# A new order for the third norm and the router, and for the convolution's modulation and value products

## The reference

```python
mod = (_silu(c) @ wmod).reshape(B, 6, 1, -1)
h = _layernorm(x, axis=-1) * (1 + ca) + sa
x = x + ga * block(h)        # ga, gb: sign kept, magnitude at least 0.25
```

```python
stats = concat([x.mean, x.std(ddof=1), x.min, x.max, norm2(x), (abs(x) < 1e-6).mean])
h = gelu(concat([xf, stats]) @ r1_w.T + r1_b)
probs = softmax(h @ r2_w.T)   # then top 2 of 32, capacity per expert
```

## Time and profile before

| | |
|---|---|
| median of 3 runs | 1381.84 us (1379.79 to 1382.64) |
| the profiled execution | 1385.09 us, span 1383.3 us |
| PE busy | 1188.5 us, 86% of the span |
| DVE, ACT, POOL busy | 922.5, 887.2, 577.3 us |
| granted TensorE clock, mean | 0.927 of full |
| first stage (norm and convolution) | 0 to 43.5 us |
| third norm and router up to its logits | 102 to 138.4 us |

### The profile page before, as it was taken

One profiled execution on the slowest core, in us unless ns is written; L12 is line 12 of the kernel. 1 busy time (PEld: TensorE's weight loads), 2 busy tenths in 40 slices (PEclk: granted clock), 3 DMA queues, 4 the chain that ended last, 5 costly groups with the idle time before them and its releaser, 6 DMA issues.

```text
span 1383.3 us, 30358 instructions
## 1 busy us (share of the span) xinstructions
PE 1188.5 (86%) x11444; PEld 713.8 (52%) x11444; DVE 922.5 (67%) x2432; ACT 887.2 (64%) x2384; POOL 577.3 (42%) x554
## 2 busy tenths in 40 slices
PE   7788038757999999999979899997899978899978
PEld 5334037753555555555534566663566643466643
DVE  3454852137989889889863699896566744666733
ACT  3564001115777777777867788885699862799961
POOL 1022024634444444444331132232788820888820
PEclk8897557979999999999999999999899999999998
DMA  9002014541000000000021122220011100011100
GB/s 335 3 0 61 9 61 134 185 125 39 1 1 1 1 1 1 1 1 1 1 107 34 45 74 71 75 79 32 16 29 29 29 15 0 22 27 25 29 14 31
DMA packets 30271, 60.36 MB, mean 44 GB/s; under 512 B 5379, under 2 KB 17163, under 8 KB 29486
## 3 DMA queue, kind: packets, MB, share of 16 engines
q1 hardware_dynamic: 28078, 56.67, 13.2%
q0 software_dynamic: 2048, 1.74, 0.5%
HBM read 45.35 MB, written 6.55 MB: 38 GB/s over the span
## 4 chain that ended last, share of the span: by engine, by line
PE 64%; ACT 14%; DVE 11%; issue 6%; another core or an unknown queue 2%; POOL 2%; DMA 1%; SPq 0%; ACTq 0%; DVEq 0%; POOLq 0%
ACT win_soft_local L1578 7%; PE bank L1114 6%; PE bank L1127 5%; PE pair L1083 4%; PE bank L1546 4%; PE bank L1527 3%; PE bank L1101 3%; PE bank L2346 3%; PE pair L1101 3%; PE pair L1086 2%; PE pair L1537 2%; PE bank L2045 2%; ACT win_sq_local L2127 2%; PE bank L1566 2%; PE bank L1134 2%
## 5 line engine op out<-in xcount | busy, mean ns | idle before, releaser
L1369 POOL TENSOR_TENSOR rope_part<-rope_part,rope_tab 128x512 f32<-128x512 f32 x64 | 81.7, 1276 | 188.8 <-DVE rope_part L1275 188.6
L2267 POOL TENSOR_TENSOR win_part<-win_part,scaled_tab 128x512 f32<-128x512 f32 x64 | 92.0, 1438 | 65.1 <-DVE win_part L2204 64.9
L1202 ACT ACTIVATE soft<-bank,neg_max 128x512 f32<-128x512 f32 (+2 forms) x192 | 100.4, 536 | 27.5 <-DVE neg_max L1283 27.3
L1578 ACT ACTIVATE win_soft_local<-bank,win_neg_max_local,rq 128x128 f32<-128x128 f32 x256 | 114.2, 475 | 0.3 <-DVE win_neg_max_local L2214 0.3
L1219 ACT ACTIVATE softT<-bank 128x512 f32<-128x512 f32 x160 | 92.5, 599 | 29.4 <-PE bank L1114 29.3
L1612 POOL TENSOR_TENSOR win_soft_alibi<-win_soft_alibi,win_inv_alibi 128x384 f32<-128x384 f32 x64 | 52.7, 826 | 138.7 <-DVE win_inv_alibi L1601 138.7
L1283 DVE CUSTOM_DVE_ANT_0 bank<-bank,att_mask 128x512 f32<-128x512 f32 (+2 forms) x192 | 92.3, 525 | 6.9 <-PE bank L1101 6.9
L1101 PE MATMUL bank<-k_rope,q_rope 64*128 64x512 f32 (+3 forms) x384 | 95.4, 473 | 1.6 <-POOL k_rope L1374 1.6
L278 POOL TENSOR_SCALAR h<-ln_norm,mod 128x512 f32<-128x512 f32 x28 | 24.2, 866 | 157.6 <-DVE ln_norm L262 157.6
L1114 PE MATMUL bank<-ident,soft 128*128 128x128 f32 x640 | 89.4, 278 | 0.6 <-ACT softT L1219 0.5
L1313 DVE TENSOR_SCALAR soft<-soft,exp_inv 128x128 f32<-128x128 f32 (+2 forms) x160 | 87.8, 596 | 1.1
(11 more groups left out here) (401 smaller groups left out, 3356.3 us busy)
## 6 DMA issues: line engine op xcount, KB each, us to landing
sloped<-in_alibi_bias SPq DMA_DIRECT2D x22, 384.0 KB, 3.3
moe_w<-in_moe_w SPq DMA_DIRECT2D x8, 960.0 KB
y_tok<-in_moe_w SPq DMA_DIRECT2D x8, 960.0 KB
v_even<-v_odd SPq DMA_DIRECT2D x32, 128.0 KB, 2.2
moe_w<-in_alibi_bias SPq DMA_DIRECT2D x10, 384.0 KB, 3.2
v_even<-v_odd SPq DMA_DIRECT2D x32, 96.0 KB, 2.2
y_dram<-zeros SPq DMA_DIRECT2D x8, 256.0 KB
htok_dram<-htok SPq DMA_DIRECT2D x2, 1024.0 KB
```

The costliest lines, as they stand in the source:

```text
L1202: nc.scalar.activation(soft[par][:, hd, TILE_AT[t]:TILE_AT[t] + keys(t)], score_bank(u, s, hd)[:, at:at + keys(t)], ACT.Exp, scale=-1.0, b ...
L1369: nc.gpsimd.tensor_tensor(rope_part[2 * piece + 1][:, :], rope_part[2 * piece + 1][:, :], rope_tab[:, 2 * piece + 1, :], ALU.mult).then_in ...
L1578: nc.scalar.activation(a["soft"][u % 2][:, j, :], tile, ACT.Exp, bias=low, scale=rq[:, u % 2, j:j + 1], accum_out=a["sum"][:, u % 2, j:j + ...
L2267: nc.gpsimd.tensor_tensor(swapped, swapped, scaled_tab[:, 2 * j + 1, :], ALU.mult) \
```

## The change

It has three parts.

1. The modulation of layer 3 leaves its place ahead of the logits: `mod_pe` for layers 1 and 2 stays there (24 instructions, bank 7), that of layer 3 (12, bank 0) follows the transposes of the probabilities, behind a wait on the first token copy. DVE turns it into gates after the bands and before the first addition to x.
2. The matmuls of the second norm are written out inside `conv_pe`: centred 0 stands behind the second value product, centred 1 behind the third, the rest behind the fourth.
3. In the third norm PE runs centred 3 and variance 2 before any token transposes; the router's channel products move from `moe_pe` to behind the transposes of their batch, into banks 1, 2, 3 and 0. ACT does no copy until `ln_root` of batch 2, and takes all copies and magnitudes before the table of the square root is loaded. DVE's statistics are in two functions, `moe_bins_dve` (bins and minimum) and `moe_stats_dve` (maximum and aggregates); bins of batch 0 stand before norm 2, its statistics before norm 3, the rest behind. POOL scales `r1_z` before the norm.

```diff
-            mod_pe(pe, bank[7], range(1, 4))
+            mod_pe(pe, bank[7], range(1, 3), first=1)
             pe.wait_ge(sem("h_ready"), 4)
...
                 last.then_inc(sem("conv_probT"), 1)
+            pe.wait_ge(sem("htok_ready"), 1)
+            mod_pe(pe, bank[0], range(3, 4), first=3)
             pe.wait_ge(sem("conv_band"), 8)
-            for b in range(B):
+
+            def taken(b):
                 pe.wait_ge(sem("htok_ready"), b + 1)
                 pe.wait_ge(sem("pv_zeroed"), b + 1)
...
                 last.then_inc(sem("pv_raw"), 1)
+
+            taken(0)
+            taken(1)
+            ln_centred(pe, 1, 0)
+            taken(2)
+            ln_centred(pe, 1, 1)
+            taken(3)
+            ln_variance(pe, 1, 0)
+            ln_centred(pe, 1, 2)
+            ln_variance(pe, 1, 1)
+            ln_centred(pe, 1, 3)
+            ln_variance(pe, 1, 2)
+            ln_variance(pe, 1, 3)
...
+            dve.wait_ge(sem("mod_raw"), 3)
+            mod_dve(dve, bank[0], 3, 4)
             for b in range(B):
                 dve.wait_ge(sem("pv_raw"), b + 1)
...
+        HID_BANK = [1, 2, 3, 0]
+
...
+        def moe_hidden_pe(pe, b):
+
+            if b == 2:
+                pe.wait_ge(sem("ln_log"), 16)
+            else:
+                pe.wait_ge(sem("ln_normed"), {0: 14, 1: 15, 3: 16}[b])
+            pe.matmul(bank[HID_BANK[b]][0:64, :], r1_c[:, :], hb(b), start=True, stop=False)
+
+        def norm3_pe(pe):
+            ln_centred(pe, 3, 0)
+            ln_centred(pe, 3, 1)
+            ln_variance(pe, 3, 0)
+            ln_centred(pe, 3, 2)
+            ln_variance(pe, 3, 1)
+            ln_centred(pe, 3, 3)
+            ln_variance(pe, 3, 2)
+            moe_tokens_pe(pe, 0)
+            pe.wait_ge(sem("moe_loaded"), 112)
+            moe_hidden_pe(pe, 0)
+            ln_variance(pe, 3, 3)
+            for b in range(1, B):
+                moe_tokens_pe(pe, b)
+                moe_hidden_pe(pe, b)
+
         def moe_pe(pe):
-            pe.wait_ge(sem("moe_loaded"), 112)
-            pe.wait_ge(sem("ln_normed"), 16)
-            for b in range(B):
-                pe.matmul(bank[b][0:64, :], r1_c[:, :], hb(b), start=True, stop=False)
...
+        def norm3_act(act):
+            nc.scalar.preload_act_table_set("natural_log_exp_and_others")
+            ln_squared(act, 3, 0)
+            ln_squared(act, 3, 1)
+            ln_root(act, 3, 0)
+            ln_squared(act, 3, 2)
+            ln_root(act, 3, 1)
+            ln_squared(act, 3, 3)
+            ln_root(act, 3, 2)
+            htok_act(act, 0, B, bank[4])
+            ln_root(act, 3, 3)
+            moe_magnitude_act(act, 0)
+            for b in range(1, B):
+                htok_act(act, b, B, bank[4 + b])
+                moe_magnitude_act(act, b)
...
             scan_pool(pool)
+            moe_spread_pool(pool)
             ln_pool(pool, 3)
...
-            mod_dve(dve, bank[7], 1, 4)
+            mod_dve(dve, bank[7], 1, 3)
...
-            ln_dve(dve, 3, ahead=lambda b: moe_stats_dve(dve, b - 2) if b >= 2 else None)
-            moe_stats_dve(dve, 2)
-            moe_stats_dve(dve, 3)
+            ln_normed(dve, 3, 0)
+            ln_normed(dve, 3, 1)
+            moe_bins_dve(dve, 0)
+            ln_normed(dve, 3, 2)
+            moe_stats_dve(dve, 0)
+            ln_normed(dve, 3, 3)
+            for b in range(1, B):
+                moe_bins_dve(dve, b)
+                moe_stats_dve(dve, b)
```

More of the change, by code:

```diff
@@ L287, in mod_act, with mod_pe @@
             nc.scalar.activation(cond_silu[:, :], cond[:, :], ACT.Silu).then_inc(sem("cond_ready"), 1)
-        def mod_pe(pe, bank_at, layers_):
+        def mod_pe(pe, bank_at, layers_, first=0):
             for l in layers_:
                 for j in range(6):
-                    at = (6 * l + j) * B
+                    at = (6 * (l - first) + j) * B
                     last = pe.matmul(bank_at[:, at:at + B], wmod[:, l, j * C:(j + 1) * C],
@@ L297, in mod_dve @@
         def mod_dve(dve, bank_at, lo, hi):
-            raw = bank_at[:, 24 * lo:24 * hi].rearrange("p (l i j b) -> p l i j b", i=2, j=3, b=B)
+            raw = bank_at[:, 0:24 * (hi - lo)].rearrange("p (l i j b) -> p l i j b", i=2, j=3, b=B)
             into = mod[:, lo:hi, :, :].rearrange("p l (i j) b -> p l i j b", j=3)
@@ L644, in moe_tokens_pe @@
             htok_pe(pe, bank[4 + b], lambda i: hh(b, 128 * i, 128))
+        def moe_hidden_pe(pe, b):
[19 more added lines that the diff above has]
+                moe_hidden_pe(pe, b)
         def moe_pe(pe):
-            pe.wait_ge(sem("moe_loaded"), 112)
-            pe.wait_ge(sem("ln_normed"), 16)
-            for b in range(B):
-                pe.matmul(bank[b][0:64, :], r1_c[:, :], hb(b), start=True, stop=False)
             for b in range(B):
                 pe.wait_ge(sem("moe_near"), b + 2)
-                pe.matmul(bank[b][0:64, :], r1_z[:, :], near_zero[:, b, :], start=False, stop=False)
+                pe.matmul(bank[HID_BANK[b]][0:64, :], r1_z[:, :], near_zero[:, b, :], start=False, stop=False)
             pe.wait_ge(sem("moe_stats"), 1)
@@ L671, in moe_pe @@
                 pe.wait_ge(sem("moe_statT_ready"), b + 1)
-                pe.matmul(bank[b][0:64, :], r1_s[0:5, :], statT[:, b, :], start=False, stop=True) \
+                pe.matmul(bank[HID_BANK[b]][0:64, :], r1_s[0:5, :], statT[:, b, :], start=False, stop=True) \
                   .then_inc(sem("moe_hid_raw"), 1)
@@ L754, in moe_out_pe, with moe_magnitude_act @@
             last.then_inc(sem("moe_out"), 1)
-        def moe_tokens_act(act, b):
-            htok_act(act, b, B, bank[4 + b])
+        def moe_magnitude_act(act, b):
+            act.wait_ge(sem("h_ready"), 12 + b + 1)
             nc.scalar.activation(near_zero[:, b, :], hb(b), ACT.Abs).then_inc(sem("moe_magnitude"), 1)
+        def norm3_act(act):
[13 more added lines that the diff above has]
+                moe_magnitude_act(act, b)
         def moe_act_engine(act):
             nc.scalar.preload_act_table(ACT.Sqrt)
-            for b in range(2, B):
-                moe_tokens_act(act, b)
             act.wait_ge(sem("moe_moments"), 2)
@@ L769, in moe_act_engine @@
                 act.wait_ge(sem("moe_hid_raw"), b + 1)
-                nc.scalar.activation(r_hid[:, b, :], bank[b][0:64, :], ACT.Gelu, bias=v("r1_b")[0:64, :]) \
+                nc.scalar.activation(r_hid[:, b, :], bank[HID_BANK[b]][0:64, :], ACT.Gelu, bias=v("r1_b")[0:64, :]) \
                   .then_inc(sem("moe_hid_ready"), 1)
@@ L790, in moe_act_engine, with moe_bins_dve @@
                       .then_inc(sem("moe_silued"), 1)
-        def moe_stats_dve(dve, b):
+        def moe_bins_dve(dve, b):
             tiles = slice(TB * b, TB * b + TB)
@@ L800, in moe_stats_dve @@
             nc.vector.tensor_reduce(stat[:, tiles, 2], rows, AX_X, ALU.min)
+        def moe_stats_dve(dve, b):
+            tiles = slice(TB * b, TB * b + TB)
+            rows = htok[:, tiles, :]
             nc.vector.tensor_reduce(stat[:, tiles, 3], rows, AX_X, ALU.max)
@@ L1001, in moe_sp, with moe_spread_pool, moe_near_pool @@
                       .then_inc(sem(f"rows_loaded{b}"), 16)
-        def moe_near_pool(pool):
+        def moe_spread_pool(pool):
             pool.wait_ge(sem("moe_loaded"), 112)
             nc.gpsimd.tensor_scalar(r1_z[:, :], r1_z[:, :], 1.0 / C, None, ALU.mult).then_inc(sem("moe_near"), 1)
+        def moe_near_pool(pool):
             for b in range(B):
@@ L2484, in _ @@
             scan_act(act)
-            ln_act(act, 3, behind=lambda b: moe_tokens_act(act, b - 1) if b in (1, 2) else None)
+            norm3_act(act)
             moe_act_engine(act)
@@ L2540, in _ @@
             conv_pe(pe)
-            ln_pe(pe, 1)
             lr_pe(pe)
@@ L2545, in _ @@
             pe.wait_ge(sem("scan_gates"), 9)
-            ln_pe(pe, 3, behind=lambda b: moe_tokens_pe(pe, b - 1) if b else None)
-            moe_tokens_pe(pe, 3)
+            norm3_pe(pe)
             moe_pe(pe)
```

## The result

Twenty runs of the changed kernel had a median of 1376.50 us, twenty of the kernel before on the same chips 1381.73: a ratio of 0.9961 (95% interval 0.9950 to 0.9971), or 5.4 us less (4.0 to 6.9). The forecast was 4.2 us less, or 1377.6. The profiled execution took 1380.7 us, span 1378.8, mean clock 0.932.

A forecast was written before the change was run, and what follows sets the result against it. The prediction took TensorE to hold 64% of the chain, its program order binding the router. 2.3 (second norm earlier) + 4.0 (router) - 2.1 (clock) = 4.2 us less: 1377.6 from the median 1381.84, range 1373.3 to 1381.3.

The forecast's parts named there:

- The logits' 2.6 us: Logits ahead of layer 3's modulation: they start at 19.9 in place of 22.48, 2.6 us earlier, range 2.4 to 2.8.
- the 2.8 named for the fast case: Logits' start: if the 24 modulation instructions ran wholly fast, conv_h would bind and the gain is 2.8 us.
- The 0.7 lost in the gap: Late modulation between probability transposes and value products: at 1.2 GHz it outlasts the idle time, 0.7 us lost, range 0 to 1.0.
- The interleave is worth nothing: Second norm's matmuls between value products: same instructions in another order, no gain as such; only the clock can change.
- The 9.7 us forecast: Value products to first variance product: 9.7 us in place of 10.1, 0.4 gained, range 1.0 lost to 0.4 gained.
- The router's 4.0 us: Third norm and router: the statistics' transposes start at 121.4 in place of 125.42, 4.0 us earlier.
- DVE as the new bound: Router: DVE's statistics, ending at 120.1, rather than PE's program order, would set the start of the statistics' transposes.
- the wait of norm 2 behind bins 0: Router on DVE: batch 2's norm, input ready at 108.85, queues behind batch 0's bins, ending 111.45; costs 1.0 us on DVE.
- signs of a wrong forecast: Forecast wrong if value products start after 35, statistics' transposes still follow a matmul, or granted clock 0.5 stands in the norm's windows.
- The 2.1 us that the clock was to take back: Statistics' transposes to last logits: clock falls 3.3 us in, stage 15.1 instead of 13.0; 2.1 lost, range 0 to 4.3.
- All else moves rigidly: Behind the router: expert loads are released by expert results, so everything later shifts unchanged, without further gain or loss.
- the upper end of the front's gain: Second norm starting 3.7 us earlier, if the fast clock is already up before the value products; the forecast was 2.3.

The follow-up runs named there:

- parts 1 and 2: Kernel before with layer 3's modulation moved and the second norm's centred products between the value products; third norm and router as before: ratio 0.9985 (0.9968 to 1.0003).
- part 3 alone: Kernel before with only the third norm and router in the new order, run twice: ratios 0.9993 and 0.9987 to the kernel before.
- the run without tests: Changed kernel with GpSimd's four near-zero tests left out, magnitudes going straight into the near-zero products: one run, 1375.44 us.
- the padded runs: Statistics product zero-filled from 5 to 128 rows: on the changed kernel 0.9937, there with DVE's batch-2 norm ahead of batch-0 bins 0.9945, on the kernel before 0.9990.
- norm 2 first: Changed kernel with DVE's norm of batch 2 ahead of the bins of batch 0: one run, 1374.88 us.
- Modulation alone: Kernel before with only layer 3's modulation moved behind the transposes of the probabilities: ratio 0.9990 (0.9972 to 1.0009).

## Why the prediction was right, step by step

**The logits' 2.6 us: 2.0 on average, and wrong in bound.** In five traces of the old front the logits came 2.76, 2.39, 1.68, 1.49 and 1.79 us behind conv_h, 2.0 on average; in nine of the new one 0.05 or 0.06. The 2.6 was right for the one trace that it was read from. I had the clock fall at 18.4 and the matmuls end last; it fell at 21.1, the 24 instructions were through (2.74 us), and conv_h was the bound. That is the 2.8 named for the fast case, 2.7 in that trace.

**The 0.7 lost in the gap: not there.** In all nine traces with the late modulation the bias-to-value stretch is 9.53 or 9.54. Twenty-four instructions fit at 2.4 GHz. In five of the nine traces the clock rose only inside the group of twelve, latest in the second trace of the changed kernel (33.4), where the value products followed at 34.38 without idle time:

```profile
32.66 1.77 PE L293 MATMUL pair<-cond_silu,wmod 128*128 128x4 f32 x12
```

There the cover was just used up. The step failed by taking one trace's low clock at that place for what holds in every run; what a group wholly at 1.2 GHz would cost no trace shows.

**Value products and second norm.** The interleave is worth nothing, as said; shown by two kernels at the same clock. The 9.7 us forecast were 8.53 and 7.20, again the clock. Besides, the sum had a batch of value products at 2.4 GHz at 1.35 us: it had spread 2.0 us over each slow batch, though the first addition to x, at 38.54, shows that the first batch took 2.4. The chain of parts 1 and 2 has 1.04 a batch. And the rise of the clock at 38.8, on which the 9.7 rests, was assumed and read from no row; in the first trace it came at 38.1, 3.1 us behind the first value product, not 4.6. The kernel before showed 8.79 in its second trace, and part 3 alone, with the old front, 7.13.

**The router's 4.0 us: right.** The forecast put the transposes at 121.4 with the scan's last x at 104.97, 16.4 us; they took 16.5 in five traces with the same DVE order, and 16.9 in two where the clock was low in the norm. DVE as the new bound was right too (the run without tests), as was the wait of norm 2 behind bins 0. Its price was 0.5 where I had 1.0, and only the norm's own time mattered. Two of my signs of a wrong forecast did appear in the first trace of the changed kernel: a granted clock of 0.5 in the norm's windows (99.6 to 103.0), which cost 0.4 us of the 4.0, and transposes that follow a matmul, the last near-zero product, by 0.15 us. The third, value products after 35, was met by 0.03 us, with conv_h 1.5 us late. None of them changes the sum by more than 0.4; as signs they were too sharp.

**The 2.1 us that the clock was to take back: the step that failed.** The stage took 12.25 to 13.55 in seven traces of the new router with the five-row product, 12.8 on average, against 13.1 in four traces of the old one. I had it at 15.1. The near-zero products one by one kept the clock up as well as those in a row, and it fell 5.1 to 6.7 us behind the transposes in seven traces (5.4 to 5.8 in four of the old order), not 3.3. What did lose it was the five-row product, as the padded runs show; I had named it and not priced it.

**The sum: right in part by luck.** From conv_h to the second norm's first logarithm five traces of the old front took 24.5 us on average (22.4 to 26.6) and nine of the new one 21.6 (21.0 to 22.5): 2.8 won, forecast 2.3. From the scan's last x to the maximum of the logits four traces of the old router took 33.5 us and seven of the new one 29.2 (both with the five-row product): 4.3 won, forecast 1.9. That makes 7.1 us by the traces, where the forecast was 4.2 and the times say 4.7 to 5.4. So the loss to the clock, which did not come, stood against a part of the gain that does not reach the end, and which I had not foreseen.

"All else moves rigidly" was the weak sentence. From the maximum of the logits to the last PE or DVE instruction the traces took 1242.3 and 1241.6 us before and 1244.4 and 1243.8 after; three more traces, of variants of the changed kernel, had 1242.4 to 1243.9, the front alone 1242.5 and 1242.3, the router alone 1239.8 and 1242.6. So 1 to 2 us may be given back behind the router, but that spread, by stages that no edit touches, is as large. Much of it arises in the expert stage: from the maximum of the logits to DVE's first rope_part the fourteen traces took 176.8 to 182.7 us, with the two of before at 180.0 and 180.5.

**Open:** why the router alone, 3.7 to 4.0 us shorter in its traces than the old one, showed 1 to 2 us in 24 runs (0.9993, 0.9987). Each interval reaches to 0.9976 or 0.9967, but all 24 runs together have a mean of 1380.5, 1.6 us under the 91 of before with an error of 0.8, so chance in the times alone is an unlikely account. Two traces stand for these 24 runs, and the first was of the fastest of its twelve (1376.88 us, their median 1380.82). For the padding on the kernel before the gap is smaller: its 3.4 us lie within its interval.

The Trainium skill's rule on transposes ("TensorE: Matmul & The Clock Gate", Part 4) weighed on the upper end of the front's gain. By the rule the full clock does not engage for them. The row of before at 28 us was weak evidence against it, since logits ran in the same stretch until 26.5. Four later traces are stronger. With norm 2 first, the logits ended at 23.8, PE had nothing but transposes from there to 31.97, and the clock rose at 32.1, with two instructions of the modulation group behind the transposes.

```profile
28.50 3.67 PE L354 MATMUL bank<-ident,prob 128*128 128x128 f32 x16 [1.09 <-DVE prob L415]
```

Modulation alone, parts 1 and 2, and the run without tests show the same within the first two or three instructions of that group (33.2, 32.3, 32.5). So for these float32 transposes the rule did not hold. The page speaks of the transpose mode; the trace records them as matmuls with the identity and does not tell the mode.

## What to carry to other kernels

A matmul group that waits for nothing should stand in a gap that a serial chain on another engine leaves, here 12 to 24 small matmuls behind the softmax, and not ahead of that chain's input. Where PE's program order is the bound, issue each product when its input exists, then look at the next engine: a ready norm in front of waiting statistics uses idle time, behind them it lengthens the packed block. Compare stretches in several traces, counted from an event that the edit can't move, before a difference of 1 or 2 us is given to an edit.

## What the runs showed of the hardware

Matmuls with five rows stream as fast as full ones (0.86 to 1.00 us for two instructions of 512 columns at 2.4 GHz, before and after the padding) but did not hold TensorE's clock in the stage that they share with 32-column logits: filling the product with zeros to 128 rows, in the same number of instructions of 512 columns, kept 2.4 GHz through a stage of 9.7 us that otherwise took 12.3 to 13.6, in two orders of the router. With it, logits matmuls of 32 columns and 64 rows between them also ran fast.

The places where the clock rises and falls move from run to run of the same program: a stretch of the same 38 PE instructions took 10.12 and 8.79 us in two traces of the kernel before, and 7.13 in the second trace of part 3, which has the same front. Stretches led by DVE repeat within 0.01 us (9.53 to 9.54 in fourteen traces).

Float32 transposes of 128x128 did not keep the clock down: in four traces it rose at 32.1 to 33.2 us behind 8 us in which PE ran only them, and for 1.1 us nothing.
